# Attention of a fused two-layer kernel: scores issued in pairs, row maxima moved in one hop, query and key rows regrouped in DRAM

## The chip, the cores and the metric

The kernel runs on one core of one Trainium2 chip. The metric is the device time of one execution in microseconds (us), of which a median over several executions is given. All data are float32 at the interface.

## The reference

Two transformer layers with modulated layer norms run over 1024 tokens (2 sequences of 512) of width 256. The change lies in the attention of the first layer, which is this (H = 256, 16 heads of 16):

```python
q_lat = hidden_states @ Wq_down.T + bq_down
kv_lat = hidden_states @ Wkv_down.T + bkv_down
q_half = q_lat @ Wq_up.T + bq_up
q = concatenate([q_half, rotary(q_half)], -1)
k_half = kv_lat @ Wk_up.T + bk_up
k = concatenate([k_half, rotary(k_half)], -1)
v = kv_lat @ Wv_up.T + bv_up
scores = einsum('bhqd,bhkd->bhqk', q, k) / sqrt(16)
out = einsum('bhqk,bhkd->bhqd', softmax(scores), v)
return out.reshape(bsz, seq, H) @ Wo.T + bo
```

After it come a mixture of 16 experts, a gated delta rule (second layer's mixer) and a mixture of 12 experts; the change doesn't touch them.

## The kernel before

The five engines' programs are written out by hand, with semaphores. Attention works in **groups**: group g is 4 heads of one of the 2 sequences, so there are NG = 8 groups. Queries and keys are each split in a high and a low part, so that float32r matmuls keep their precision.

**The rows.** TensorE makes q and k with features on the partitions. `parts_out` (SP queue) writes the high and low parts, four [128, 512] pieces at a time, to the DRAM scratch `part_scratch`. `k_rows` and `q_rows` read them back by head: for a group they fill two tiles [128, 2, 512], Kt and Qt, in which each half of the partitions (`jb` = 0 or 1, from partition 0 or 64) holds two heads, 16 rows to a part (high, low, high for keys; high, high, low for queries), 48 rows in all. A group takes eight such DMAs: four of 32 rows (two parts at once, 128 KB) and four of 16 rows (one part, 64 KB). A row is 4096 bytes. `piece_rows` gives the DRAM side; its pattern is

```python
rows = part_dram[b, n, t // 2, part:part + end - r].rearrange("x (d t o j) n -> (x d) t o (j n)", t=2, j=HP, o=2)
```

where x counts the parts, d the 16 rows of a head, and t, o, j the heads.

**Two score passes.** First pass (`scores`): TensorE makes scores [128 queries, 512 keys] of one head into one of three PSUM banks in turn (`SLOTS`), and VectorE reduces them to a negated maximum per query (`max_of`). There are 16 such scores n to a group, 128 in all. The two halves jb use different rows of the array, and n alternates between them. When a group's 16 maxima are there, VectorE splits them in a bfloat16 high and low part (`mpart`), TensorE turns them (`max_rows`), VectorE copies them to `max_sb`, and the SP queue writes `max_sb` to the DRAM scratch `max_scratch`, waits until that has landed, and reads it back into two more rows of Qt (`maxima_in`). Second pass (`scores_t`): scores with keys on the partitions, in which rows 48 and 49 subtract the maximum; ScalarE takes exp of two heads at once, and TensorE multiplies with the values (`values`).

**The order.** The first FIRST = 26 scores come ahead of everything else; between them stand `up` and `values_in` matmuls and, later, `warm(2, 6)`, two matmuls that do nothing. Then come the groups: each of 8 steps p has a pair of `scores_t`, with the first-pass scores of a later group (`ahead`) between them. `values` of key tile kt come at p = 2 kt + 3. MAX_LAG = 4 says how many scores after a group's last one its `max_rows` stands.

**The SP queue** is written out in the order of the program: the input loads; `parts_out` and the rows of each group; `maxima_in(0)` after the rows of group 2; `maxima_in(1)` after those of group 4; `maxima_in(2)` after those of group 6; then the rows of group 7, the ones rows, `wmod[1]` (1536 KB) and the other `maxima_in`. The rows of query group 0 go by ScalarE's queue.

Of the kernel before, what the change touches and what calls it, by code (L numbers as in the profile page):

```python
# [21 lines left out]
F32 = mybir.dt.float32  # L22
BF16 = mybir.dt.bfloat16
# [6 lines left out]
P = 128  # L30
# [68 lines left out]
FIRST = HG * TB + 10  # L99
MAX_LAG = 4  # L100

# [42 lines left out]
def program(nc, a, out):  # L144
    with ExitStack() as ctx:
        def sb(name, shape, dt=F32):
            return ctx.enter_context(nc.sbuf_tensor(name, shape, dt))
# [38 lines left out]
        small = sb("small", [P, 256])  # L186
        mpart = sb("mpart", [P, 2, 2, NH], BF16)
        max_sb = sb("max_sb", [2 * NH, 2, P])
        ring0 = sb("ring0", [P, 2, W0C])
# [314 lines left out]
        part_dram = nc.dram_tensor("part_scratch", (B, 2, 2, 2, P, S), F32, kind="Internal").ap()  # L504
        max_dram = nc.dram_tensor("max_scratch", (2 * NH, P), F32, kind="Internal").ap()
        ab_dram = nc.dram_tensor("ab_scratch", (2 * NH, TOK), F32, kind="Internal").ap()
# [74 lines left out]
        def piece_rows(n, b, t, r, end, jb):  # L581

            part = (QP, KP)[n][r]
            rows = part_dram[b, n, t // 2, part:part + end - r].rearrange("x (d t o j) n -> (x d) t o (j n)", t=2, j=HP, o=2)
            return rows[:, t % 2, jb]

# [29 lines left out]
        def _(sp):  # L616
# [29 lines left out]
            def maxima_in(g):  # L646

                sp.wait_ge(free_sem(("maxima", g)), uses(("maxima", g)))
                if g:
                    sp.wait_ge(s["max_in"], 32 * g)  # L650
                load("max_out", max_dram, max_sb[:, g % 2, :])
                sp.wait_ge(s["max_out"], 16 * (g + 1))
                for jb in range(2):
                    load("max_in", head_rows(Qt[g // TB][g % TB], jb, KR, KR + 2).bitcast(F32),
                         max_dram.rearrange("(h o j t) q -> h o j (t q)", h=2, j=HP, o=2)[:, jb])

# [23 lines left out]
            for t in (2, 3):  # L680
                ones_rows(sp, 1, t, "ones_late")
            load("ld_mod1", wmod[1], a["wmod"][1])
            for g in range(3, NG):
                maxima_in(g)

            def chunk0(n, k):
# [225 lines left out]
        def _(act):  # L912
# [69 lines left out]
            for g in range(NG):  # L982
                for p in range(2 * TB):
                    act.wait_ge(s["s2"], 2 * TB * g + p + 1)
                    if TB * g + p // 2 >= 2:
                        act.wait_ge(s["av"], TB * g + p // 2 - 1)
                    lo = p // 2 % 2 * HG + p % 2 * 2
                    act.activation(pexp[:, lo:lo + 2, :], psum[:, 2 + p % 2 * 2:4 + p % 2 * 2, :], ACT.Exp,  # L988
                                   scale=HD ** -0.5).then_inc(s["exp"], 1)
                    if g and p == 1:  # L990
                        out_of_psum(g - 1)
                    if (g, p) == (0, 3):
                        high_turned(1)
# [247 lines left out]
        def _(pe):  # L1241
# [77 lines left out]
            def modulate_rows(layer):  # L1319
                pe.wait_ge(s["ld_mod1"], 16 * (layer + 1))  # L1320
                for n in range(2 + layer):
                    for k in range(KD):
                        ins = pe.matmul(bank[MOD_BANKS[layer]][n * Q:n * Q + B, :], ccol[:, layer * KD + k, :],
                                        wmod[layer][:, k, 512 * n:512 * n + 512], start=(k == 0), stop=(k == KD - 1))
                ins.then_inc(s["mod_mm"], 1)
# [61 lines left out]
            def max_rows(g):  # L1387

                pe.wait_ge(s["mpart"], g + 1)
                next_bank("maxima", g)  # L1390
                pe.transpose(bank_b[slot(("maxima", g))][0:2 * NH, 0:P],
                             mpart[:, g % 2, :, :].rearrange("p h n -> p (h n)"), identb[:, :])\
                    .then_inc(full_sem(("maxima", g)), 1)
# [12 lines left out]
            mod_turned(0)  # L1406
            warm(12, 0)
            pe.wait_ge(s["mod_in"], 1)
            for n in range(FIRST):
                scores_and_maxima(n)  # L1410
                if 1 <= n <= 4:
                    if n == 4:
                        pe.wait_ge(s["v_in"], 2)
                    up(1, UP_ORDER[n - 1])
                if n in (6, 8):
                    if n == 8:
                        high_made(pe, 1, 0, 0)
                    values_in(2 + (n - 6) // 2)
                if n >= 10:
                    if n == 10:  # L1420
                        pe.wait_ge(s["up_copy"], 3)
                    warm(2, 6)
            pe.wait_ge(s["up_copy"], 4)
            high_made(pe, 1, 0, 1)
            pe.wait_ge(s["v_in"], NT // 2)
            for g in range(NG):
                for p in range(2 * TB):
                    if p == 0:
                        pe.wait_ge(s["max_in"], 32 * (g + 1))
                        if g == 0:  # L1430
                            pe.wait_ge(s["ones"], 2)
                            pe.wait_ge(s["ones_in"], 16 * 12)
                        if g == TB + 2:
                            pe.wait_ge(s["ones_late"], 64)
# [5 lines left out]
                    if last_maxima_due(g, p):  # L1440
                        max_rows(NG - 1)
                    if p > 1 and p % 2:
                        values(g, p // 2 - 1)
                    elif g and p == 1:
                        values(g - 1, TB - 1)
# [430 lines left out]
        def _(dve):  # L1876
# [105 lines left out]
            def max_of(n):  # L1982
                g, (jj, jb, qt) = n // (HG * TB), head_of(n)
                own, at = nm[:, g % 2, :], (HP * jb + jj) * TB + qt
                dve.tensor_reduce(own[:, at:at + 1], full("scores", n), AX, ALU.max,  # L1985
                                  negate=True).then_inc(free_sem(("scores", n)), 1)
                if n % (HG * TB) == HG * TB - 1:
                    for last in (n - 2, n - 1, n):
                        dve.wait_ge(free_sem(("scores", last)), uses(("scores", last)))
                    ch.link(dve.tensor_copy(mpart[:, g % 2, 0, :], own))  # L1990
                    dve.tensor_tensor(mpart[:, g % 2, 1, :], own, mpart[:, g % 2, 0, :],
                                      ALU.subtract).then_inc(s["mpart"], 1)

            def max_rows(g):
                full("maxima", g)
                if g >= 2:
                    dve.wait_ge(s["max_out"], 16 * (g - 1))
                dve.tensor_copy(max_sb[:, g % 2, :], bank_b[slot(("maxima", g))][0:2 * NH, 0:P])\
                   .then_inc(free_sem(("maxima", g)), 1)

# [691 lines left out]
def lay_out(i):  # L2692
# [15 lines left out]
    up = np.zeros((P, 4, P), f)  # L2708
    turned = np.arange(P).reshape(2, HG, HD).transpose(2, 0, 1).reshape(-1)
    for n, w in enumerate((i["L0_attn_Wq_up"], i["L0_attn_Wk_up"])):  # L2710
# [99 lines left out]
```

## Time and profile before

| | us |
|---|---|
| median of 3 runs | 839.17 |
| lowest and highest | 837.61, 839.66 |
| the profiled execution's own time | 833.2 |
| its span in the profile | 830.9 |
| PE busy | 769.2 (93%) |
| DVE busy | 538.7 (65%) |
| ACT busy | 262.4 (32%) |
| POOL busy | 212.6 (26%) |

The span runs from the first to the last instruction of the profiled execution. PE is TensorE, DVE VectorE, ACT ScalarE, POOL GpSimd; SPq is the queue that issues DMAs. In a timeline row stand the start, the duration of the merged piece, the engine, the line and the operation, and in brackets how long the engine sat idle before it and who ended that. The granted clock of TensorE is 0.96 of full speed over the span. The attention of the first layer lies between about 22 and 160 us.

### The profile page before, as it was taken

How to read it: one execution, taken by the hardware profiler on the slowest of the kernel's cores; microseconds unless marked ns; L12 is line 12 of the kernel's file. 1: busy time of each engine (PE TensorE's matmuls, PEld its weight loads, DVE VectorE, ACT ScalarE, POOL GpSimd, SP SyncE). 2: the span in 40 equal slices, each digit the busy share in tenths (PEclk: the TensorE clock that was granted, in tenths of full speed). 3: DMA queues.
4: the chain of work that ended last, by engine and by line, in shares of the span. 5: the costliest groups of instructions: out<-in, count | busy, mean ns of one | idle time of the engine just before them, and what ended most of it. 6: DMA issues, size and time to landing. Idle time of an engine off the chain costs nothing. (4 is left out here: it accounts for less than half of the span.)

```text
span 830.9 us, 11650 instructions
## 1 busy us (share of the span) xinstructions
PE 769.2 (93%) x4039; PEld 567.0 (68%) x4051; DVE 538.7 (65%) x1312; ACT 262.4 (32%) x417; POOL 212.6 (26%) x202
## 2 busy tenths in 40 slices
PE   8999899999999999999999498998876899999995
PEld 4433343467788888887545387777752899999995
DVE  6577797187655445554789999999478353434345
ACT  2425567534344343433573112021230100000000
POOL 4610000021232222321011000777001253434331
PEclk9998899989999999999999799999987999999997
DMA  7646201001111112131031504400013899999972
GB/s 240 173 131 174 88 4 42 1 23 35 39 57 38 57 38 58 38 117 55 7 108 51 215 1 127 103 0 1 1 52 126 319 345 344 332 354 332 353 256 87
DMA packets 39374, 102.24 MB, mean 123 GB/s; under 512 B 6112, under 2 KB 17632, under 8 KB 38944
## 3 DMA queue, kind: packets, MB, share of 16 engines
q1 hardware_dynamic: 34864, 91.63, 33.0%
q0 software_dynamic: 3888, 9.08, 3.0%
q10 hardware_dynamic: 576, 0.92, 0.4%
q8 instruction: 27, 0.44, 0.2%
q14 instruction: 19, 0.16, 0.1%
HBM read 84.12 MB, written 17.56 MB: 122 GB/s over the span
## 5 line engine op out<-in xcount | busy, mean ns | idle before, releaser
L1494 PE MATMUL psum<-xr,wr 128*128 128x512 f32 x600 | 147.1, 395 | 1.3 <-DVE arena L2144 1.0
L1494 PEld LDWEIGHTS psum<-xr,wr 128*128 128x128 f32 x600 | 114.4, 191 | 26.4 <-issue 2.5
L832 POOL TENSOR_TENSOR wr<-ring,wr 128x512 fp32r<-128x512 f32 (+1 forms) x50 | 54.8, 1115 | 252.1 <-ACT wr L1016 148.3
L1985 DVE TENSOR_REDUCE small<-psum 128x1 f32<-128x512 f32 x128 | 81.4, 684 | 21.9 <-PE psum L1354 21.6
L1810 PEld LDWEIGHTS psum<-arena 128*128 128x128 f32 x700 | 83.5, 192 | 3.2 <-issue 1.5
L1810 PE MATMUL psum<-arena 128*128 128x128 f32 x700 | 83.9, 275 | 1.1 <-ACT arena L1220 1.1
L1820 PE MATMUL psum<-arena 128*128 128x256 f32 x350 | 81.3, 379 | 0.0
L2607 DVE TENSOR_SCALAR arena<-psum,arena 128x256 f32<-128x256 f32 x35 | 16.9, 484 | 94.0 <-PE psum L1820 94.0
L1505 PE MATMUL psum<-hr,wr 128*128 128x512 f32 x300 | 76.6, 391 | 0.9 <-DVE hr L2079 0.9
L988 ACT ACTIVATE arena<-psum 128x1024 f32<-128x1024 f32 x64 | 62.8, 1022 | 44.0 <-PE psum L1363 43.7
L2107 DVE TENSOR_TENSOR hid<-hid,psum 128x512 f32<-128x512 f32 x50 | 34.4, 687 | 57.0 <-ACT hid L1022 56.8
L1820 PEld LDWEIGHTS psum<-arena 128*128 128x128 f32 x350 | 63.8, 190 | 7.2
L1505 PEld LDWEIGHTS psum<-hr,wr 128*128 128x128 f32 x300 | 56.2, 188 | 13.0 <-issue 1.3
L1220 ACT ACTIVATE arena<-psum 128x256 f32<-128x256 f32 x35 | 13.4, 383 | 153.3 <-PE psum L1799 153.3
L2079 DVE TENSOR_TENSOR hr<-hid,hr 128x512 fp32r<-128x512 f32 x50 | 35.0, 700 | 34.0 <-ACT hr L1029 33.8
L1029 ACT ACTIVATE hr<-hid 128x512 fp32r<-128x512 f32 x50 | 31.6, 632 | 78.5 <-DVE hid L2130 68.4
L887 POOL DMA_INDIRECT arena<-h_scratch,arena x35 | 36.2, 1033 | 70.8 <-DVE arena L2580 60.5
L1354 PE MATMUL psum<-k_rows,q_rows 48*128 48x512 f32 x128 | 52.3, 488 | 1.4
L893 POOL DMA_INDIRECT z_scratch<-arena x32 | 31.6, 987 | 81.3 <-DVE arena L2607 81.3
L2639 DVE TENSOR_SCALAR arena<-psum,arena 128x128 f32<-128x128 f32 x175 | 48.2, 342 | 3.6 <-PE psum L1810 3.6
L1363 PE MATMUL psum<-q_rows,k_rows 50*128 50x512 f32 x128 | 42.2, 464 | 3.1 <-DMA q_rows<-max_scratch 2.5
L1269 PE MATMUL psum<-sel,identb 128*128 128x512 bf16 x157 | 43.6, 403 | 0.5 <-issue 0.2
(391 smaller groups left out, 1195.3 us busy)
## 6 DMA issues: line engine op xcount, KB each, us to landing
arena<-in_w1u SPq DMA_DIRECT2D x35, 642.5 KB, 5.8
arena<-in_w1d SPq DMA_DIRECT2D x35, 640.0 KB, 5.5
ring<-in_w SPq DMA_DIRECT2D x25, 384.0 KB, 3.0
part_scratch<-arena SPq DMA_DIRECT2D x16, 256.0 KB, 2.8
z_scratch<-w_a SPq DMA_DIRECT2D x4, 768.0 KB, 7.2
arena<-z_scratch SPq DMA_DIRECT2D x8, 384.0 KB, 6.3
k_rows<-part_scratch SPq DMA_DIRECT2D x16, 128.0 KB, 2.7
qkv_scratch<-arena SPq DMA_DIRECT2D x4, 512.0 KB, 2.8
```

What stands on the lines that cost most here:

```text
L832: pool.tensor_tensor(wr0[:, k, LO, part], ring0[:, k, part], wr0[:, k, HI, part], ALU.subtract).then_inc(s["w0_lo"], 1)
L887: pool.indirect_dma_start(xg[:, r % NXG, :], None, h_dram, bass.IndirectOffsetOnAxis(ap=tok_i[:, r:r + 1], axis=0))\
L988: act.activation(pexp[:, lo:lo + 2, :], psum[:, 2 + p % 2 * 2:4 + p % 2 * 2, :], ACT.Exp, scale=HD ** -0.5).then_inc(s["exp"], 1)
L1269: pe.matmul(bank[spare][:, :], identb[:, :], sel0[:, :], start=True, stop=True)
L1354: pe.matmul(to, head_rows(Qt[b][t], jb, 0, KR)[:, jj, tile(qt)], head_rows(Kt[b][t], jb, 0, KR)[:, jj, :], start=True, stop=True)\
L1363: ins = pe.matmul(bank[2 + 2 * pair + jb][:, :], head_rows(Kt[b][t], jb, 0, KR + 2)[:, pair, tile(kt)], head_rows(Qt[b][t], jb, 0, KR + 2) ...
L1494: ins = pe.matmul(bank[2 * b + m][:, :], wr0[:, k, w, lo:lo + P], xr[:, x, f, half(b)], start=(f == 0 and (w, x) == PARTS[0]), stop=(f == ...
L1505: ins = pe.matmul(bank[4 + 2 * m + b][:, :], wr0[:, k, w, lo:lo + P], hr[:, b, x, :], start=(first and (w, x) == PARTS[0]), stop=(last and ...
L1810: ins = pe.matmul(bank[2 + r % 2 * 3 + k // 2][:, tile(k % 2)], wup1[:, r % NW, lo:lo + P], xgT[:, r % 2, f, :], start=(f == 0), stop=(f = ...
L1820: ins = pe.matmul(bank[1][:, 0:D], hact[:, r % 2, tile(k)], wdn1[:, r % NW, k * D:(k + 1) * D], start=(k == 0), stop=(k == NC1 - 1))
L1985: dve.tensor_reduce(own[:, at:at + 1], full("scores", n), AX, ALU.max, negate=True).then_inc(free_sem(("scores", n)), 1)
L2639: ins = dve.tensor_scalar(hact[:, r % 2, tile(k)], bank[2 + r % 2 * 3 + k // 2][:, tile(k % 2)], bias, 0.0, ALU.add, ALU.max)
```

## The change

It has five parts.

- The first 26 scores come in pairs n, n + 1 (the two halves of the array), with one `up` or `values_in`, or three `warm` matmuls, after each pair; `warm(12, 0)` ahead of them becomes `warm(6, 0)`, and the wait for `mod_in` moves to n = 4.
- The maxima are turned in float32 straight from `nm`, VectorE writes the high and low part from PSUM to `max_sb`, and four DMAs (half by part) carry them from SBUF to Qt. `max_scratch` and its wait are gone; MAX_LAG is 3.
- The features are ordered anew in the weights (`turned`, in `lay_out`), so that the two heads of one half lie in 64 KB without gaps per part in `part_scratch`.
- `values` of key tile kt come at p = 2 kt + 2, between the two halves of the next key tile, and `out_of_psum` one step earlier.
- `wmod[1]` is loaded in two halves, after `maxima_in(3)` and `maxima_in(4)`.

```diff
-MAX_LAG = 4
+MAX_LAG = 3
...
-        mpart = sb("mpart", [P, 2, 2, NH], BF16)
-        max_sb = sb("max_sb", [2 * NH, 2, P])
+        max_sb = sb("max_sb", [NH, 2, 2, P], F32R)
...
-            rows = part_dram[b, n, t // 2, part:part + end - r].rearrange("x (d t o j) n -> (x d) t o (j n)", t=2, j=HP, o=2)
-            return rows[:, t % 2, jb]
+            rows = part_dram[b, n, t // 2, part:part + end - r].rearrange("x (t o d j) n -> x d t o (j n)", t=2, j=HP, o=2)
+            return rows[:, :, t % 2, jb]
...
                 if g:
-                    sp.wait_ge(s["max_in"], 32 * g)
-                load("max_out", max_dram, max_sb[:, g % 2, :])
-                sp.wait_ge(s["max_out"], 16 * (g + 1))
+                    sp.wait_ge(s["max_in"], 64 * g)
                 for jb in range(2):
-                    load("max_in", head_rows(Qt[g // TB][g % TB], jb, KR, KR + 2).bitcast(F32),
-                         max_dram.rearrange("(h o j t) q -> h o j (t q)", h=2, j=HP, o=2)[:, jb])
+                    for part in (HI, LO):
+                        load("max_in", head_rows(Qt[g // TB][g % TB], jb, KR + part, KR + part + 1)
+                             .rearrange("p j n -> p (j n)").bitcast(F32),
+                             max_sb[jb * NH // 2:(jb + 1) * NH // 2, g % 2, part, :].bitcast(F32))
...
-            load("ld_mod1", wmod[1], a["wmod"][1])
             for g in range(3, NG):
                 maxima_in(g)
+                if g - 3 < KD:
+                    load("ld_mod1", wmod[1][:, g - 3], a["wmod"][1, :, g - 3])
...
-                    if g and p == 1:
+                    if g and p == 0:
                         out_of_psum(g - 1)
...
             def max_rows(g):
-                pe.wait_ge(s["mpart"], g + 1)
-                next_bank("maxima", g)
-                pe.transpose(bank_b[slot(("maxima", g))][0:2 * NH, 0:P],
-                             mpart[:, g % 2, :, :].rearrange("p h n -> p (h n)"), identb[:, :])\
+                for n in range(HG * TB * (g + 1) - 3, HG * TB * (g + 1)):
+                    pe.wait_ge(free_sem(("scores", n)), uses(("scores", n)))
+                pe.transpose(next_bank("maxima", g)[0:NH, 0:P], nm[:, g % 2, :], ident[:, :])\
                     .then_inc(full_sem(("maxima", g)), 1)
...
-            warm(12, 0)
-            pe.wait_ge(s["mod_in"], 1)
-            for n in range(FIRST):
+            warm(6, 0)
+            for n in range(0, FIRST, 2):
                 scores_and_maxima(n)
-                if 1 <= n <= 4:
+                scores_and_maxima(n + 1)
+                if n < 8:
...
-                    warm(2, 6)
+                    warm(3, 6)
...
-                    if p > 1 and p % 2:
+                    if p and p % 2 == 0:
                         values(g, p // 2 - 1)
-                    elif g and p == 1:
+                    elif g and p == 0:
                         values(g - 1, TB - 1)
...
             def max_rows(g):
-                full("maxima", g)
+                turned = full("maxima", g)[0:NH, 0:P]
                 if g >= 2:
-                    dve.wait_ge(s["max_out"], 16 * (g - 1))
-                dve.tensor_copy(max_sb[:, g % 2, :], bank_b[slot(("maxima", g))][0:2 * NH, 0:P])\
-                   .then_inc(free_sem(("maxima", g)), 1)
+                    dve.wait_ge(s["max_in"], 64 * (g - 1))
+                ch.link(dve.tensor_copy(max_sb[:, g % 2, HI, :], turned))
+                dve.tensor_tensor(max_sb[:, g % 2, LO, :], turned, max_sb[:, g % 2, HI, :].bitcast(F32),
+                                  ALU.subtract).then_inc(free_sem(("maxima", g)), 1)
...
-    turned = np.arange(P).reshape(2, HG, HD).transpose(2, 0, 1).reshape(-1)
+    turned = np.arange(P).reshape(2, 2, HP, HD).transpose(0, 1, 3, 2).reshape(-1)
```

On the SP queue, this is what stands between the row DMAs of group 2 (k_rows_59, q_rows_51) and of group 3 (k_rows_60) before; the shapes are those of the destination:

```order
L602 DMA k_rows_59<-part_scratch 32x1024
L602 DMA k_rows_59<-part_scratch 16x1024
L602 DMA k_rows_59<-part_scratch 32x1024
L602 DMA k_rows_59<-part_scratch 16x1024
L608 DMA q_rows_51<-part_scratch 16x1024
L608 DMA q_rows_51<-part_scratch 32x1024
L608 DMA q_rows_51<-part_scratch 16x1024
L608 DMA q_rows_51<-part_scratch 32x1024
L618 DMA max_scratch<-max_sb 32x128
L618 DMA q_rows_49<-max_scratch 2x1024 x2
L602 DMA k_rows_60<-part_scratch 32x1024
```

and in the changed kernel:

```order
L600 DMA k_rows_59<-part_scratch 32x1x1024
L600 DMA k_rows_59<-part_scratch 16x1024
L600 DMA k_rows_59<-part_scratch 32x1x1024
L600 DMA k_rows_59<-part_scratch 16x1024
L606 DMA q_rows_51<-part_scratch 16x1024
L606 DMA q_rows_51<-part_scratch 32x1x1024
L606 DMA q_rows_51<-part_scratch 16x1024
L606 DMA q_rows_51<-part_scratch 32x1x1024
L616 DMA q_rows_49<-max_sb 1x8x128 x4
L600 DMA k_rows_60<-part_scratch 32x1x1024
```

The place of the maxima of group 0 (q_rows_49) is the same, behind the rows of group 2. The DMAs of 32 rows have one more dimension, since x and d no longer make one stride: the DRAM side is now 2 parts, 65536 elements apart, of 16 rows, 1024 elements apart; before it was 32 rows, 4096 elements apart. The 16-row DMAs read 16 adjacent rows.

On TensorE, two key tiles of group 2 (keys k_rows_59; L1363 is `scores_t`, L1354 `scores`, L1376 `values`) before:

```order
L1363 MATMUL psum<-q_rows_51,k_rows_59 128x512
L1354 MATMUL psum<-k_rows_60,q_rows_52 128x512
L1363 MATMUL psum<-q_rows_51,k_rows_59 128x512
L1354 MATMUL psum<-k_rows_60,q_rows_52 128x512
L1363 MATMUL psum<-q_rows_51,k_rows_59 128x512
L1354 MATMUL psum<-k_rows_60,q_rows_52 128x512
L1363 MATMUL psum<-q_rows_51,k_rows_59 128x512
L1354 MATMUL psum<-k_rows_60,q_rows_52 128x512
L1376 MATMUL psum<-arena 17x512 x4
```

and in the changed kernel (L1362, L1353 and L1375 are the same three):

```order
L1362 MATMUL psum<-q_rows_51,k_rows_59 128x512
L1353 MATMUL psum<-k_rows_60,q_rows_52 128x512
L1362 MATMUL psum<-q_rows_51,k_rows_59 128x512
L1353 MATMUL psum<-k_rows_60,q_rows_52 128x512
L1375 MATMUL psum<-arena 17x512 x4
L1362 MATMUL psum<-q_rows_51,k_rows_59 128x512
L1353 MATMUL psum<-k_rows_60,q_rows_52 128x512
L1362 MATMUL psum<-q_rows_51,k_rows_59 128x512
L1353 MATMUL psum<-k_rows_60,q_rows_52 128x512
```

`values` moved from behind both halves of a key tile to between them; what it multiplies is the exp of the key tile before.

## Rows read from the trace of the kernel before

**Rows 1.** The head of the page.

```profile
span 830.9 us, 11650 instructions
```

**Rows 2.** Timeline, TensorE: the first scores_t (L1363) of groups 0 to 6.

```profile
54.03 0.49 PE L1363 MATMUL psum<-q_rows,k_rows 50*128 50x512 f32 x1
...
68.67 0.50 PE L1363 MATMUL psum<-q_rows,k_rows 50*128 50x512 f32 x1
...
81.33 0.49 PE L1363 MATMUL psum<-q_rows,k_rows 50*128 50x512 f32 x1 [0.69 <-DMA q_rows<-max_scratch]
...
95.07 0.50 PE L1363 MATMUL psum<-q_rows,k_rows 50*128 50x512 f32 x1 [1.80 <-DMA q_rows<-max_scratch]
...
109.26 0.49 PE L1363 MATMUL psum<-q_rows,k_rows 50*128 50x512 f32 x1
...
122.08 0.50 PE L1363 MATMUL psum<-q_rows,k_rows 50*128 50x512 f32 x1
...
133.98 0.50 PE L1363 MATMUL psum<-q_rows,k_rows 50*128 50x512 f32 x1
```

**Rows 3.** One line's instructions, VectorE L1985 from 29 to 54 us, and its idle time.

```profile
L1985 DVE TENSOR_REDUCE small<-psum x26: 678/691/692, 30.0 to 53.6; 128x1 f32<-128x512 f32 x26
...
  PE psum L1354: 8.9, 18
```

**Rows 4.** Timeline, the SP queue: start, us, line, DMAs.

```profile
22.26 8.80 SPq L602 DMA_DIRECT2D k_rows<-part_scratch  x8
...
48.55 0.30 SPq L618 DMA_DIRECT2D max_scratch<-max_sb  x1
49.94 0.55 SPq L618 DMA_DIRECT2D q_rows<-max_scratch  x2
...
85.41 0.40 SPq L618 DMA_DIRECT2D arena<-in_wmod  x1
88.98 0.33 SPq L618 DMA_DIRECT2D max_scratch<-max_sb  x1
93.18 0.52 SPq L618 DMA_DIRECT2D q_rows<-max_scratch  x2
```

**Rows 5.** What the SP queue waited for, 20 to 145 us: in total, times, longest.

```profile
SPq L618 <- DMA max_scratch<-max_sb: 13.1, 8, 3.9
...
SPq L602 <- DMA q_rows<-part_scratch: 5.4, 1, 5.4
```

**Rows 6.** DMA issues: queue, count, KB each, median us to landing where told.

```profile
k_rows<-part_scratch SPq DMA_DIRECT2D x16, 128.0 KB, 2.7
...
q_rows<-max_scratch SPq DMA_DIRECT2D x16, 8.0 KB
k_rows<-hid POOLq DMA_DIRECT2D x12, 8.0 KB, 5.4
...
k_rows<-hid SPq DMA_DIRECT2D x4, 8.0 KB
```

**Rows 7.** Stretches; the last three columns are PEclk, DMA share, GB/s.

```profile
50.98:51.15 0.17, 0.17 (x2) 0.02 (x1) 0.17 (x1) 0.00 (x0) 0.00 (x0) 1.00 0.12 50
50.98:51.38 0.40, 0.40 (x2) 0.18 (x1) 0.40 (x1) 0.00 (x0) 0.00 (x0) 1.00 0.13 41
52.00:53.00 1.00, 1.00 (x4) 0.30 (x3) 0.72 (x2) 0.00 (x0) 0.00 (x0) 1.00 0.74 205
56.00:57.00 1.00, 1.00 (x5) 0.58 (x5) 1.00 (x3) 1.00 (x2) 0.00 (x0) 1.00 1.05 402
...
96.00:102.50 6.50, 6.50 (x28) 2.04 (x25) 4.67 (x10) 4.31 (x5) 0.00 (x0) 0.50 0.00 0
```

**Rows 8.** Timeline of the first key tile of group 5: exp, values, next scores_t.

```profile
122.85 1.94 ACT L988 ACTIVATE arena<-psum 128x1024 f32<-128x1024 f32 x2 [0.76 <-PE psum L1363]
...
123.80 1.05 PE L1376 MATMUL psum<-arena 128*17 128x512 f32 x8
...
124.78 0.50 PE L1363 MATMUL psum<-q_rows,k_rows 50*128 50x512 f32 x1
```

More of the change, by code:

```diff
@@ L504, in program @@
         part_dram = nc.dram_tensor("part_scratch", (B, 2, 2, 2, P, S), F32, kind="Internal").ap()
-        max_dram = nc.dram_tensor("max_scratch", (2 * NH, P), F32, kind="Internal").ap()
         ab_dram = nc.dram_tensor("ab_scratch", (2 * NH, TOK), F32, kind="Internal").ap()
@@ L1319, in modulate_rows @@
             def modulate_rows(layer):
-                pe.wait_ge(s["ld_mod1"], 16 * (layer + 1))
+                pe.wait_ge(s["ld_mod1"], 16 * (1 + KD * layer))
                 for n in range(2 + layer):
@@ L1406, in _ @@
             mod_turned(0)
-            warm(12, 0)
-            pe.wait_ge(s["mod_in"], 1)
-            for n in range(FIRST):
+            warm(6, 0)
+            for n in range(0, FIRST, 2):
                 scores_and_maxima(n)
-                if 1 <= n <= 4:
+                scores_and_maxima(n + 1)
+                if n < 8:
                     if n == 4:
+                        pe.wait_ge(s["mod_in"], 1)
+                    if n == 6:
                         pe.wait_ge(s["v_in"], 2)
-                    up(1, UP_ORDER[n - 1])
-                if n in (6, 8):
-                    if n == 8:
+                    up(1, UP_ORDER[n // 2])
+                elif n < 12:
+                    if n == 10:
                         high_made(pe, 1, 0, 0)
-                    values_in(2 + (n - 6) // 2)
-                if n >= 10:
-                    if n == 10:
+                    values_in(2 + (n - 8) // 2)
+                else:
+                    if n == 12:
                         pe.wait_ge(s["up_copy"], 3)
-                    warm(2, 6)
+                    warm(3, 6)
             pe.wait_ge(s["up_copy"], 4)
@@ L1428, in _ @@
                     if p == 0:
-                        pe.wait_ge(s["max_in"], 32 * (g + 1))
+                        pe.wait_ge(s["max_in"], 64 * (g + 1))
                         if g == 0:
@@ L1986, in max_of @@
                                   negate=True).then_inc(free_sem(("scores", n)), 1)
[L1987 to L1992, printed above, removed]
             def max_rows(g):
-                full("maxima", g)
+                turned = full("maxima", g)[0:NH, 0:P]
                 if g >= 2:
-                    dve.wait_ge(s["max_out"], 16 * (g - 1))
-                dve.tensor_copy(max_sb[:, g % 2, :], bank_b[slot(("maxima", g))][0:2 * NH, 0:P])\
-                   .then_inc(free_sem(("maxima", g)), 1)
+                    dve.wait_ge(s["max_in"], 64 * (g - 1))
+                ch.link(dve.tensor_copy(max_sb[:, g % 2, HI, :], turned))
+                dve.tensor_tensor(max_sb[:, g % 2, LO, :], turned, max_sb[:, g % 2, HI, :].bitcast(F32),
+                                  ALU.subtract).then_inc(free_sem(("maxima", g)), 1)
             def normalise(g):
```

## The prediction

> **What bounds the kernel now.** I read the timeline first, because the change lies in one stage. The span is 830.9 us [rows 1], and the first `scores_t` of the groups stand at 54.0, 68.7, 81.3, 95.1, 109.3, 122.1 and 134.0 us [rows 2]. What the reader should see is the spacing: group 5 takes 133.98 - 122.08 = 11.90 us with nothing to wait for, groups 2 and 3 begin after waits of 0.69 and 1.80 us for the maxima from DRAM, and group 3 takes 14.19 us, since from 96 to 102.5 us the granted clock was 0.50 [rows 7], that is 1.2 GHz, after the idle 1.80 us. So a restart at the low clock costs 14.19 - 11.90 = 2.3 us. Ahead of group 0 lie 26 single scores, 29.5 to 54.0 us; VectorE needs 0.69 us for each and sat idle 8.9 us between them, waiting for scores [rows 3]. TensorE bounds that stretch and the groups. All that follows attention only starts later or earlier with it.
>
> The transfers are next. The rows of group 0 are issued at 22.26 us, and the SP queue waits 5.4 us for them before it issues those of group 1 [rows 4, 5]. The maxima of group 0 go out at 48.55 us, 1.39 us later the queue may read them back, and their first bytes move at 50.98 us, 1.04 us after that issue [rows 4, 7]. In the case of group 3 the first hop took from 88.98 to 93.18 us, 4.2 us, because 1536 KB had been issued at 85.41 us [rows 4]: a small transfer stands behind the large ones ahead of it on its queue. That matters below.
>
> **The part that decides: how many DMA engines a row transfer gets.** In rows 7 the stretch 50.98 to 51.38 us holds only the two reads of maxima, each of two rows of 4096 bytes. The DMA share is 0.13, which is 2 engines of 16, and 41 GB/s: the two rows of a transfer go side by side on two engines, and the second transfer goes after the first on the same two, though 14 are free. These transfers, and the ones rows from the SP queue, are also the only ones for which no landing time is told, while those from GpSimd's queue have one [rows 6]; I read this as another number of completions than 16. So a transfer is dealt out once, by its outermost count. The 32-row transfers had the outermost count 32 on both sides. After the change x and d make no single stride, and the DRAM side is 2 x 16 rows, outermost count 2. The trace has no transfer of 32 rows in two blocks. The bounds are 2 engines (nearest in outermost count) and 16 (nearest in size). I take 2, since the two reads behind one another show that size and free engines play no role.
>
> The Trainium skill, "DMA: Bandwidth & Descriptors", section "Why a DMA increments its semaphore by 16 and not by 1", says that a DMA runs on the largest number up to 16 that divides the slowest dimension of both sides, on hardware queues the lowest-numbered engines. By that rule 32-row transfers get 2 engines and the sum below holds; without it the first rival does. This case's 0.13 of 16 agrees as far as it goes.
>
> **Price of a row.** On two engines 50 GB/s gives 25 GB/s each, 0.164 us for 4096 bytes; over both transfers 41 GB/s gives 0.20; in the contended stretch 52 to 53 us 205 GB/s on 0.74 x 16 engines gives 0.24 [rows 7]. I take 0.165 us, the uncontended one, since 14 engines will be mostly idle; 0.20 is kept for the range. One group: four 32-row transfers put 16 rows on each of the two engines, four 16-row ones put 1 row: 68 x 0.165 = **11.2 us**. One `parts_out` of 4 x 128 rows of 2048 bytes puts 32 rows on each; 402 GB/s on 1.05 x 16 engines gives 0.086 us a row [rows 7]: **2.75 us**. An issue takes 1.05 us to its first row, and a landing about 0.3 us (estimate).
>
> **The sum**, along the SP queue's order. Group 0's rows: 22.26 + 1.04 + 11.2 = 34.5, landed 34.8 (before, some 29.4 by the 5.4 us wait). Group 1's, first row 35.9, done 47.1; parts of the other head pair behind them 49.8, landed 50.1. Group 2's rows 51.2 to 62.4; the maxima of group 0, behind them, 62.7, so group 0 begins at 62.7 instead of 54.0. Group 3's rows 73.6, parts 76.4 (landed 76.7), group 4's rows 77.7 to 88.9, maxima of group 1 at 89.2 (68.7 before). Parts 91.7, group 5's rows 102.9, group 6's 114.1, **maxima of group 2 at 114.4 instead of 81.3: +33.1 us**. TensorE has by then stood idle some 12 us and restarts at 1.2 GHz: group 2 takes 11.9 + 2.3 = 14.2 and ends at 128.6; group 7's rows are in at 125.3 and the maxima of group 3 at 125.6, so group 3 begins at 128.6, +33.5. From there no row is owed. Group 3 before held a low-clock restart that now has no cause: -2.3. So +31.2.
>
> The other parts. **Pairs** would save TensorE time in the first 26 scores, but these now wait for rows and maxima: 0. **One hop** saves 1.4 us a group and the two waits of 0.69 and 1.80 us; groups 0 to 2 wait for the queue instead, and group 3's wait is gone in the sum already: 0. VectorE loses two small operations a group and gains one in another place: 0, hidden behind TensorE, worth at most some 0.2 us a group. `max_rows` at MAX_LAG 3 stands inside a pair and holds up one `scores_t` by up to one reduction, 0.6 us a group at most, 0 at least; taken as 0. **wmod** in halves is behind maxima: 0. **Values between the halves**: exp starts 0.77 us after its half's first matmul (122.08 to 122.85) and takes 0.97 [rows 2, 8], ready 1.75 us after it; two halves of four matmuls occupy TensorE 1.72 us (122.08 to 123.80), and values 0.98 (to 124.78). Values used to find their exp ready; now they wait for the half just before, so a key tile takes 1.80 + 0.98 = 2.78 instead of 2.70. Over some 14 key tiles +1.1; in the last group and a half, where no first-pass scores fill the halves, about 0.3 us for each of 6 tiles. I take +2 (0 to 4).
>
> Sum: 31.2 + 2 = **+33 us** on the profiled execution's 833.2 (span 830.9), so 866. That execution was 6.0 us under the median 839.17; on the median the forecast is **872 us**.
>
> **Rivals.**
> - *All 16 engines work on the 2 x 16 rows (the other side: faster).* Then the rows stay hidden. Pairs bring the first 26 scores to VectorE's pace [rows 3], 26 x 0.69 = 17.9 instead of 24.6 us: -6.7; the waits -0.69 and -1.80; the restart -2.3; values +2: -9.5, so **830 us**. It decides at about four engines: 4 x 8 + 4 = 36 rows, 5.9 us a group, is already less than a group's 11.9. For it: TensorE idles nowhere in the trace for rows of this size, and 128 KB landed in 2.7 us [rows 6]. Against it: the two-row stretch. 12%.
> - *Two engines, but the maxima overtake.* They use eight partitions and could travel on other engines. Then only the rows count: group 4's at 88.9 are needed in group 2, group 7's at 125.3 in group 5; groups 0 and 1 start late by 4 to 8 us, and little is regained: about **843 us**. Against it: the 4.2 us of group 3's first hop. 5%.
> - *Two engines, slow rows.* At 0.20 us, 0.035 x 68 x 7 groups = +17 more: **889 us**; at 0.24, 908. Rows read side by side could be as slow as in the second read of maxima. I count 0.20 as the edge of the forecast's own range, and 5% beyond.
> - The forecast itself: 78%, with its own range 856 to 890.
>
> **How the numbers follow.** The likeliest case gives 872. The range 854 to 892 leaves out the first two rivals and the slowest rows. A measurement of this kernel can tell about 0.3%, 2.5 us, from no change. Faster: the first rival, 0.12. Same: a remainder between the first two, 0.02. Slower: 0.86.
>
> **What would show it.** Right: between 24 and 125 us the DMA share near 0.13, and some 45 to 50 GB/s; the SP queue waits over 10 us for group 0's rows; TensorE's first `scores_t` at about 63, 89, 114 and 129 us, the waits put down to `q_rows<-max_sb`, granted clock 0.50 after each; from group 3 on the spacing of before, about 12 us; key tiles of 2.8 instead of 2.7 us. The 32-row transfers should have no landing told. Wrong: 32-row transfers that land in 3 us and groups that begin ahead of 54 us. If rows take 11 us a group and the maxima land early all the same, the queue order was misread.

## The result, and the profile after

The changed kernel took **882.1 us** (median of 4 runs, 879.26 to 883.69), the kernel before 838.39 (4 runs, 831.53 to 839.66). The ratio is 1.0535, 95% interval 1.0471 to 1.0599. The profiled execution took 881.46 us with a span of 879.2, beside 833.2 and 830.9 [rows 1]: +48.3 us. The forecast was 872 on the median, +33 on the profiled execution: the right sign and mechanism, 10 us short on the median and 15 us on the execution.

The head of its page, and the granted clock and the DMA share in 40 slices of 22 us each, in tenths:

```profile
span 879.2 us, 11628 instructions
...
PEclk8785568999899999999999979999996999999997
DMA  6222311010011111111303150430001799999973
```

Slices 4 to 6, 66 to 132 us, hold the clock's dip (5, 5, 6): groups 0 to 2 of attention. Behind attention only single slices stand at 7 or 6, three of them; the page of before has three such slices too (7). I then read the same views in the same order as before. First the timeline of TensorE (start, us, engine, line, operation; behind it the idle time and what ended it), for the first `scores_t` of groups 0, 1, 2 and 3 and the last one of all:

```profile
70.51 0.76 PE L1362 MATMUL psum<-q_rows,k_rows 50*128 50x512 f32 x1 [9.26 <-DMA q_rows<-max_sb]
...
98.10 0.79 PE L1362 MATMUL psum<-q_rows,k_rows 50*128 50x512 f32 x1 [12.13 <-DMA q_rows<-max_sb]
...
124.31 0.79 PE L1362 MATMUL psum<-q_rows,k_rows 50*128 50x512 f32 x1 [11.23 <-DMA q_rows<-max_sb]
...
140.73 0.40 PE L1362 MATMUL psum<-q_rows,k_rows 50*128 50x512 f32 x1
...
202.12 0.50 PE L1362 MATMUL psum<-q_rows,k_rows 50*128 50x512 f32 x2
```

Against [rows 2] group 0 is 16.5 us late, group 1 29.4, group 2 43.0, group 3 45.7. Three waits for `q_rows<-max_sb` hold 32.6 us; behind group 3 nothing is owed. From group 3 to the last `scores_t` it is 61.4 us; before, it was 57.7 (95.07 to 152.73), so 3.7 us more come there. 45.7 + 3.7 = 49.4 at the end of attention, 48.3 at the end of the program: the rest only moved.

The waits of TensorE and of the SP queue (in total, times, longest), 20 to 170 us:

```profile
PE psum L1362 <- DMA q_rows<-max_sb: 32.6, 3, 12.1
...
PE psum L1353 <- DMA q_rows<-part_scratch: 7.5, 1, 7.5
```
```profile
SPq L616 <- DVE max_sb L1993: 29.3, 4, 10.4
SPq L600 <- DMA part_scratch<-arena: 22.7, 4, 9.1
SPq L600 <- DMA q_rows<-part_scratch: 11.2, 1, 11.2
```

The queue waits 11.2 us for group 0's rows, where it waited 5.4 [rows 5]. Stretches (length; busy us and count of PE, PEld, DVE, ACT and POOL; granted clock, DMA share, GB/s):

```profile
11.00:18.00 7.00, 5.72 (x12) 2.71 (x12) 3.60 (x10) 1.45 (x2) 0.00 (x0) 0.51 0.59 171
...
28.50:37.50 9.00, 2.34 (x12) 0.97 (x10) 0.17 (x1) 1.41 (x3) 2.49 (x2) 0.86 0.13 53
...
35.00:48.00 13.00, 9.59 (x15) 3.14 (x16) 4.44 (x7) 3.22 (x5) 3.05 (x3) 0.50 0.37 129
...
68.00:104.00 36.00, 21.34 (x81) 8.29 (x85) 13.76 (x24) 12.18 (x14) 2.50 (x2) 0.50 0.33 116
...
121.00:137.00 16.00, 12.66 (x49) 4.53 (x49) 6.72 (x12) 5.61 (x6) 0.00 (x0) 0.50 0.11 44
```

The second of these stretches, 28.5 to 37.5 us, is the main one: only rows move, at a DMA share of 0.13, two engines of 16, and 53 GB/s: 26.5 GB/s each, 0.155 us for a row of 4096 bytes. TensorE meanwhile has nothing to do for some 7 us (31 to 38 us). And each wait is paid for twice, with the idle time and with slow work behind it: the clock is 0.50 (1.2 GHz) from 35 to 48, 68 to 104 and 121 to 137 us.

### The profile page after: what moved, and what is told of

It reads as the page before. It is cut to its first block and busy times, and to the rows that moved or that the text cites. A ratio compares the mean times of both kernels' runs of the same rounds, so it can differ in the third digit from the quotient of the medians.

```text
span 879.2 us, 11628 instructions
## 1 busy us (share of the span) xinstructions
PE 780.0 (89%) x4034; PEld 569.9 (65%) x4034; DVE 537.1 (61%) x1304; ACT 262.4 (30%) x417; POOL 212.8 (24%) x202
## 5 line engine op out<-in xcount | busy, mean ns | idle before, releaser
L1985 DVE TENSOR_REDUCE small<-psum 128x1 f32<-128x512 f32 x128 | 80.3, 682 | 63.5 <-PE psum L1353 63.4
L1362 PE MATMUL psum<-q_rows,k_rows 50*128 50x512 f32 x128 | 47.9, 510 | 32.6 <-DMA q_rows<-max_sb 32.6
L1362 PEld LDWEIGHTS psum<-q_rows,k_rows 50*128 50x128 f32 x128 | 23.3, 220 | 64.0 <-DMA q_rows<-max_sb 24.5
L1353 PE MATMUL psum<-k_rows,q_rows 48*128 48x512 f32 x128 | 54.9, 550 | 8.3 <-DMA q_rows<-part_scratch 7.5
L2634 DVE TENSOR_SCALAR arena<-psum,arena 128x128 f32<-128x128 f32 x175 | 48.3, 342 | 3.7 <-PE psum L1810 3.7
```

The costliest lines, as they stand in the source:

```text
L1353: pe.matmul(to, head_rows(Qt[b][t], jb, 0, KR)[:, jj, tile(qt)], head_rows(Kt[b][t], jb, 0, KR)[:, jj, :], start=True, stop=True)\
L1362: ins = pe.matmul(bank[2 + 2 * pair + jb][:, :], head_rows(Kt[b][t], jb, 0, KR + 2)[:, pair, tile(kt)], head_rows(Qt[b][t], jb, 0, KR + 2) ...
L2634: ins = dve.tensor_scalar(hact[:, r % 2, tile(k)], bank[2 + r % 2 * 3 + k // 2][:, tile(k % 2)], bias, 0.0, ALU.add, ALU.max)
```

## The experiments

Eleven kernels ran, one of them twice, in four sets, each beside runs of the kernel before on the same chip. The medians of before were 837.4, 839.2, 837.4 and 837.9 us; each ratio is to the one of its own set, and between sets the ratios compare better than the medians.

### Which part costs: the layout undone, transfers split, the layout alone

**old_layout**: the changed kernel with the DRAM layout of before.

```
-  rearrange("x (t o d j) n -> x d t o (j n)", ...); rows[:, :, t % 2, jb]
+  rearrange("x (d t o j) n -> (x d) t o (j n)", ...); rows[:, t % 2, jb]
-  turned = np.arange(P).reshape(2, 2, HP, HD).transpose(0, 1, 3, 2)
+  turned = np.arange(P).reshape(2, HG, HD).transpose(2, 0, 1)
```

> The changed kernel with one part undone: the parts lie in DRAM as before, so that a row transfer of 32 rows has one outermost count of 32 again; one hop for the maxima, pairs, and values between the halves stay. Theory (the number of DMA engines of the row transfers is the whole cause): about 832 us (830 from the first rival of the prediction, and the values between the halves may cost 2 more), the DMA share over 0.5 while rows arrive, and the first scores_t of groups 0 to 3 near 49 to 54, 63 to 67, 76 to 80 and 89 to 93 us. Rival 1 (the maxima in four small transfers from SBUF to SBUF are slow by themselves, 2.7 us for their issues): the groups still wait for q_rows<-max_sb, 845 us or more. Rival 2 (values between the halves cost a lot): key tiles stay at 2.85 us and the total is about 838 to 842.

836.1 us, ratio 0.9993 (0.9963 to 1.0023). The whole loss is gone, and so the layout is its cause (with what it makes of the transfers; the next kernel parts the two); but nothing is gained either, where 832 was expected. The trace says why:

```profile
49.23 0.47 PE L1362 MATMUL psum<-q_rows,k_rows 50*128 50x512 f32 x1 [0.57 <-DMA q_rows<-max_sb]
...
65.04 0.79 PE L1362 MATMUL psum<-q_rows,k_rows 50*128 50x512 f32 x1 [5.05 <-DMA q_rows<-max_sb]
...
81.45 0.40 PE L1362 MATMUL psum<-q_rows,k_rows 50*128 50x512 f32 x1
```
```profile
55.77 0.28 DVE L1993 TENSOR_TENSOR max_sb<-psum,max_sb 16x128 fp32r<-16x128 f32 x1
...
56.40 1.72 SPq L600 DMA_DIRECT2D k_rows<-part_scratch  x4
58.16 2.90 SPq L606 DMA_DIRECT2D q_rows<-part_scratch  x4
61.19 2.69 SPq L616 DMA_DIRECT2D q_rows<-max_sb  x4
```

Group 0 begins 4.8 us earlier than before, as the pairs promise. But group 1's maxima, in SBUF at 56.05 us, are issued at 61.19, behind eight row loads for group 4, and their four issues take 2.7 us where the two reads of before took 0.55 [rows 4]. TensorE waits 5.05 us and runs group 1 at the low clock. That is rival 1 of the expectation in another form: the maxima go out late, by their place and by the length of their issues. The transfers themselves are not slow, TensorE goes 1.2 us after the end of the last issue (63.88 us). What the place of the values costs, rival 2, comes below.

**split_16**: the contiguous layout stays; every 2 x 16-row transfer goes out as two of 16 rows.

```
-KRUN = ((0, 2), (2, 3))          QRUN = ((0, 1), (1, 3))
+KRUN = ((0, 1), (1, 2), (2, 3))  QRUN = ((0, 1), (1, 2), (2, 3))
```

> The changed kernel, its contiguous DRAM layout kept, but each transfer of two parts (2 x 16 rows) is issued as two transfers of 16 rows, twelve a group instead of eight. Theory (outermost count 2 is the cause, not the layout): within 2 us of the kernel with the old layout, about 832 us; four more issues a group at about 0.55 us each on the SP queue, 2.2 us, are hidden. Rival (contiguous rows in DRAM are slow to read, whatever the number of engines): stays at about 882 us, or clearly above 850. Rival (the queue's issue time becomes the bound): 835 to 840 us, with groups 0 to 2 late by 2 to 4 us.

841.8 us, ratio 1.0042 (1.0014 to 1.0070). 40 of the 44 us are gone with the layout in place: it is not contiguous DRAM that is slow, it is the form 2 x 16. The remaining 5.7 us over old_layout fit the third theory: the SP queue issues from 48.6 to 71.0 us with only some 1.4 us of waits, and the maxima of group 1 go out at 68.28 instead of 61.19. Of these 7.1 us, 2.2 are a later start of this execution (its first `part_scratch` issue stands at 21.12 us against 18.91; see the last section), so some 5 are the queue's.

**before_new_layout**: the kernel before with the layout alone (the same two edits, the other way round).

> The kernel before with one part of the change alone: the contiguous DRAM layout, whose 32-row transfers have 2 x 16 rows. Theory (this part alone makes the loss): 878 to 890 us, since the maxima still go out to DRAM and come back, each hop behind rows that run on two engines; the difference to the kernel before is 40 to 50 us. Rival (the loss comes from the layout together with the four small transfers of the maxima, or with the new place of the values): under 865 us.

895.0 us, ratio 1.0697 (1.0641 to 1.0753): +57.6, above the expected 878 to 890. Here both hops of the maxima stand behind two-engine rows: group 1's go out at 91.39 us and may be read back only at 101.04.

```profile
91.39 0.33 SPq L618 DMA_DIRECT2D max_scratch<-max_sb  x1
101.04 0.52 SPq L618 DMA_DIRECT2D q_rows<-max_scratch  x2
```

So the change's other parts together are worth some 13 us beside this layout, and as a whole they add nothing to the loss. The 9.7 us between these two rows are a hop that the change doesn't have, so I take most of the 13 us to be that hop; no run has it alone.

### How the loss grows with the rows on the fullest engine

**split_q_only** applies the `QRUN` edit alone. A group then has two transfers of 2 x 16 rows and eight of 16 rows (two for the keys, six for the queries): 2 x 16 + 8 = 40 rows on each of the two fullest engines. The expectations here and for blocks_8 say 38; they left the keys' own 16-row transfers out.

> The changed kernel with only the query side's transfers of two parts issued as two of 16 rows; the key side's stay 2 x 16. A group then puts 2 x 16 + 6 = 38 rows on each of the two lowest engines instead of 68, about 6.3 to 7.2 us at 0.165 to 0.19 us a row, less than the 12 us of a group's work. Theory (there is a threshold: rows cost only what does not fit beside a group's work; the prediction put it at about 36 rows): worked along the SP queue, maxima of group 1 at about 71 us instead of 67, of group 2 at about 87 instead of 84, nothing owed from there on: 838 to 846 us. Rival (the loss is proportional to the rows on the fullest engine): 882 minus 30/64 of about 48, which is 859 us.

855.6 us, ratio 1.0224 (1.0175 to 1.0274). **blocks_8** lays the parts out in between, with 4 blocks `h` of 4 dimensions `d`:

```
-  rearrange("x (t o d j) n -> x d t o (j n)", ...)
+  rearrange("x (h t o d j) n -> (x h) d t o (j n)", ..., h=4)
-  turned = ....reshape(2, 2, HP, HD).transpose(0, 1, 3, 2)
+  turned = ....reshape(2, 2, HP, 4, HD // 4).transpose(3, 0, 1, 4, 2)
```

> The changed kernel with a DRAM layout between the two: the 16 dimensions of a head in 4 blocks of 4, heads between the blocks. A 32-row transfer has an outermost count of 8 (blocks of 4 rows), a 16-row transfer one of 4. Theory of the outermost count: 8 and 4 engines work, 4 rows each, so a group puts 32 rows on the fullest engine (68 in the change, 38 in split_q_only, 12 in old_layout), and the DMA share while rows run is 0.25 to 0.5. If the loss is proportional to the rows on the fullest engine (836 at 12, 855.6 at 38, 882 at 68, so 0.8 us a row): 852 us. If there is a threshold near 36 rows, as the prediction had it: 838 to 842 us. If a transfer runs either on two engines or on all: 836 or 882 us.

846.6 us, ratio 1.0074 (1.0039 to 1.0109), and in its stretches, while rows are the only transfers:

```profile
30.50:31.00 0.50, 0.50 (x4) 0.20 (x3) 0.17 (x1) 0.40 (x1) 0.50 (x1) 1.00 0.43 156
31.50:32.00 0.50, 0.37 (x2) 0.00 (x0) 0.00 (x0) 0.00 (x0) 0.50 (x2) 1.00 0.22 82
```

0.43 and 0.22 of 16 engines are some 7 and 3.5 engines. From 29.5 to 32.5 us all half microseconds lie between 0.22 and 0.43, so neither two engines nor all; I read them as 8 and 4 with gaps, which is what outermost counts of 8 and 4 give. The Trainium skill, "DMA: Bandwidth & Descriptors", section "Why a DMA increments its semaphore by 16 and not by 1", takes the largest number up to 16 that divides the slowest dimension of both sides; the 0.13 of the changed kernel agrees, and these two shares fit it.

The series, by rows of a group on the fullest engine, is 12 rows 836.1 us, 32 rows 846.6, 40 rows 855.6, 68 rows 882.1. That is 0.53 us a row between the first two, 1.1 in the next step (two more issues a group are in it) and 0.95 in the last. (blocks_8 ran in a set whose kernel before was 1.7 us slower; by the ratios the first two steps are 0.34 and 1.6.) 846.6 lies between the two theories, 852 and 842, and split_q_only at 855.6 is far nearer to the proportional 859 than to the threshold's 838 to 846. **The prediction took anything under 36 rows a group to be free, and that is wrong**: at 32 rows the ratio is 1.0074 against 0.9993 at 12, with intervals that don't meet. Rows that fit beside a group's 12 us still delay the start of groups 0 to 2, for there each link waits for the one before: rows, first-pass scores, maxima, and these behind the next rows. In blocks_8 TensorE waits 0.4, 10.2 and 3.1 us for the maxima of groups 0, 1 and 2 and not for those of group 3, in split_q_only 6.8, 5.0 and 5.2 us.

**new_layout_maxima_first** asks whether the place of the maxima in the queue alone could hide slow rows. On SP, in the changed kernel:

```
             load("ld_g", consts[:, :], a["consts"])
+            maxima_in(1)
             parts_there(1, 0)
             both_rows(1, 0)
-            maxima_in(1)
...
             both_rows(1, 1)
+            maxima_in(2)
             parts_there(1, 1)
             both_rows(1, 2)
-            maxima_in(2)
             both_rows(1, 3)
```

> The changed kernel, its row transfers on two engines, with only the order of the SP queue changed: maxima of group 1 ahead of the rows of group 4, maxima of group 2 ahead of the rows of group 6. Theory (most of the loss in groups 1 and 2 is the maxima's place behind 12 to 14 us of rows that nobody needs yet, not the rows themselves): group 1 begins near 86 us instead of 98 and group 2 near 100 to 105 us instead of 124, total 858 to 866 us. Rival (rows themselves are needed as they come): under 5 us of gain, 877 us or more.

878.6 us, ratio 1.0459 (1.0414 to 1.0503): my theory fell. Its first half holds, group 1 begins at about 83.9 us, 14 earlier than in the change. Then

```profile
111.85 0.79 PE L1362 MATMUL psum<-q_rows,k_rows 50*128 50x512 f32 x1 [15.37 <-DMA q_rows<-max_sb]
...
135.32 0.79 PE L1362 MATMUL psum<-q_rows,k_rows 50*128 50x512 f32 x1 [9.90 <-DMA q_rows<-max_sb]
```

group 2 and group 3 wait the longer, since their maxima stand behind all the rows that were passed over: those of group 3 are issued at 122.37 us, behind the rows of group 7. So group 3 begins at 135.3 us, only 5.4 earlier than in the change (140.7, where it didn't wait), and groups 3 to 7 need 62.6 us behind it instead of 61.4. With slow rows the order of the queue moved the wait and hardly shortened it: 3.5 us by the medians, 6 by the ratios.

### The place of the values, and a version that beats both

**old_layout_values_back** is old_layout with the values behind both halves again, on TensorE and, for what leaves PSUM, on ACT:

```
-                    if p and p % 2 == 0:
+                    if p > 1 and p % 2:
                         values(g, p // 2 - 1)
-                    elif g and p == 0:
+                    elif g and p == 1:
                         values(g - 1, TB - 1)
...
-                    if g and p == 0:
+                    if g and p == 1:
                         out_of_psum(g - 1)
```

> The kernel with the old DRAM layout, and the values again after both halves of the next key tile (PE and ACT order of before); one hop, pairs and MAX_LAG 3 stay. Theory (the place of the values costs time from group 3 on: 61.3 us from group 3's start to the last scores_t in old_layout against 57.7 before, with 3.3 us of PE waits for the exp): that stretch falls back to about 57.7 us, total 832.5, 3.6 us under old_layout. Rival (the longer stretch comes from max_rows standing inside a pair at MAX_LAG 3, or from the four issues of the maxima): the stretch stays at about 61 us, total 836.

831.0 us, ratio 0.9905 (0.9869 to 0.9941): 5.1 us under old_layout, in two different sets (7.4 by the ratios). Group 3's start to the last `scores_t` is 54.9 us (89.60 to 144.50) instead of 61.3. Before, it was 57.7 with a restart of 2.3 in it, so the new place costs some 6 us. The same stretch is 54.9 us in all three variants of the change with the values behind the halves, and 60.8 to 62.6 us in the change and its six variants with the values between them. The last group shows it best; first the changed kernel, then this one:

```profile
191.57 1.05 PE L1375 MATMUL psum<-arena 128*17 128x512 f32 x8 [0.36 <-ACT arena L987]
...
193.62 0.50 PE L1362 MATMUL psum<-q_rows,k_rows 50*128 50x512 f32 x2
194.48 1.05 PE L1375 MATMUL psum<-arena 128*17 128x512 f32 x8 [0.36 <-ACT arena L987]
...
196.33 1.02 ACT L987 ACTIVATE arena<-psum 128x1024 f32<-128x1024 f32 x1 [0.98 <-PE psum L1362]
```
```profile
136.98 1.05 PE L1375 MATMUL psum<-arena 128*17 128x512 f32 x8
...
138.83 1.94 ACT L987 ACTIVATE arena<-psum 128x1024 f32<-128x1024 f32 x2
...
139.47 1.05 PE L1375 MATMUL psum<-arena 128*17 128x512 f32 x8
```

From `values` to `values`, a key tile takes 2.91 us against 2.49. Between the halves the values wait 0.36 us for exp, and exp then waits 0.98 us for the half behind the values: each engine waits for the other once a tile.

**maxima_first_values_back** adds the SP order of new_layout_maxima_first to it.

> As old_layout_values_back, and on the SP queue the maxima of groups 1 and 2 are moved ahead of the row loads of groups 4 and 6. Theory (in old_layout group 1's maxima are in SBUF at 56.0 us but issued at 61.2 us behind eight row loads, TensorE idles 5.0 us and restarts at 1.2 GHz, about 4 us more in that group): both go, group 1 begins near 61.5 us and group 2 near 74 us, total about 825 us (822 to 829), under both kernels. Rival (something else delays group 1, for instance the four issues of 0.65 us each and their landing): group 1 begins at 64 us or later and the total stays at 830 us or more.

**822.5 us, ratio 0.9800 (0.9766 to 0.9834)**, under both kernels. A second measurement, **best_again**:

> maxima_first_values_back a second time. All theories: 822 to 826 us, ratio 0.98 to 0.985 to the kernel before. If the first measurement had mostly caught executions whose start ran at the full clock, 825 to 827 us. Its profile should show group 0 at 48 to 57 us, the earlier value when the granted clock is 1.00 from 11 to 18 us.

823.4 us (819.38 to 825.96), ratio 0.9808 (0.9776 to 0.9840). TensorE's and SP's rows of that profile:

```profile
PE psum L1362 <- DMA q_rows<-max_sb: 1.8, 3, 0.6
PE psum L1353 <- DMA q_rows<-part_scratch: 1.5, 1, 1.5
```
```profile
59.66 3.02 SPq L616 DMA_DIRECT2D q_rows<-max_sb  x4
62.72 1.82 SPq L600 DMA_DIRECT2D k_rows<-part_scratch  x4
```

The maxima go ahead of group 4's rows, group 1 begins at 64.91 us, no wait is over 0.6 us for them, and attention's last `scores_t` is at 144.94 us, 7.8 us earlier than before. The profiled executions differ by 8.1 us (825.09 and 833.2), the medians by 14.5; no trace shows where the rest arises.

What the new queue order brings beside old_layout_values_back is 8.5 us by the medians of one set. Their traces don't show it: the profiled execution of old_layout_values_back was its fastest (824.87 us); there TensorE waited only 0.78 us for group 1's maxima, and its last `scores_t` stands at 144.50 us. So the gain is measured and its way, fewer waits for maxima, is argued.

Three more kernels take this version apart.

**before_pairs** is the kernel before with the change's loop over the first 26 scores:

```
-            for n in range(FIRST):
-                scores_and_maxima(n)
+            for n in range(0, FIRST, 2):
+                scores_and_maxima(n)
+                scores_and_maxima(n + 1)
...
```

> The kernel before with one part of the change alone: its first 26 scores go out in pairs, the other TensorE work of that stretch between the pairs. The prediction priced pairs at 6.7 us if nothing else binds (26 reductions at VectorE's 0.69 us instead of 24.6 us). Theory: group 0 begins 5 to 6 us earlier (54.0 to about 48.5 us), groups 1 and 2 then wait more for their maxima, which stand behind eight row loads and take two hops; 1 to 4 us are left at the end, 834 to 837 us beside 838. Rival (all of it arrives): 832 us.

835.8 us, ratio 0.9977 (0.9947 to 1.0007). Nothing that can be told apart. In the trace group 0 begins 1.4 us earlier than before, though this execution started 3.6 us later (first `part_scratch` issue at 21.55 us against 17.99), and the groups then wait longer for their maxima, 0.88, 1.96 and 1.08 us for groups 1 to 3 against 0, 0.69 and 1.80 [rows 2].

**best_singles** is maxima_first_values_back with that loop of before, one score at a time.

> maxima_first_values_back without the pairs: its first 26 scores one at a time as before, so the rest is one hop and the new queue order. Theory (the 16.7 us under the kernel before come from pairs, 6, from the maxima's one hop and place, 4 to 6, and from restarts at 1.2 GHz that fall away, 2 to 4, and these add up): 828 to 830 us. Rival (pairs bring nothing since the later groups regain it): 823 us; other rival (only pairs count): 837 us.

830.3 us, ratio 0.9907 (0.9875 to 0.9939). So pairs are worth some 7 to 8 us here, and at most some 4 in the kernel before (the interval's lower end): a gain at the front arrived only in the kernel in which the next wait had been moved too.

**maxima_first** is maxima_first_values_back with the values between the halves, the edit above undone.

> maxima_first_values_back with the values between the halves again. Theory (their place costs 3.5 to 5 us, by old_layout against old_layout_values_back): 826 to 828 us against 822.5. Rival (with the maxima early the place of the values does not matter): 823 us.

830.3 us, ratio 0.9911 (0.9875 to 0.9947), 7 to 8 us over it. Their place matters, whether the maxima are early or not.

## Why the prediction was right in direction and short in size

- **Two engines for 2 x 16 rows: right.** Share 0.13, 53 GB/s, and undoing it by layout or by splitting takes the loss away. The sign that I gave, a share near 0.13 from 24 to 125 us, holds only where rows move alone; over that whole stretch it is 0.27, since other transfers run in it. That all missing landing times would mark such transfers was a poor sign: the 64 KB transfers of 16 rows had none in the changed kernel either, yet split_16 shows them to be fast.
- **0.165 us a row: right when rows move alone (0.155), short along the path.** Group 0 was forecast at 62.7 and began at 70.5. Of these 7.8 us, 2.4 are a late start (SP's first row issue at 24.66 us instead of 22.26, with the granted clock at 0.51 from 11 to 18 us, where [rows 4]'s execution had 1.00). The other 5.4 are rows: group 2's are issued at 54.55 us, forecast 50.1, and the maxima behind them let TensorE go at 70.51, 16.0 us later, where 12.6 were forecast. The next two groups took 27.6 and 26.2 us against 26.5 and 25.2. In all 7.5 us. Spread over the 7 x 68 rows on that way it would be 0.18 us a row instead of 0.165, and 0.21 in group 2's part (3.4 us over 68 rows), where several transfers are under way; I had 0.20 as an edge. Whether the rows themselves are slower there or the issues and landings around them was not settled.
- **Group 2 at the low clock: 16.4 us instead of 14.2.** I took the cost of one restart from a group that had waited 1.8 us. Here the clock stayed at 0.50 until 137 us, and TensorE was busy only 12.7 of the 16 us. +2.2.
- **Values between the halves: the term that was most wrong.** Forecast +2 (0 to 4), though its own two terms, 1.1 and 6 x 0.3, add up to 2.9; measured about 6 by the stretch behind group 3, 5.1 and 7.8 by medians. I had priced the wait of TensorE for exp and not ACT's wait for TensorE behind it. The 2.3 us saved on group 3's restart were right in kind (12.4 us against 14.2), so the net was +3.7 and not -0.3: +4.0.
- Together 2.4 + 7.5 + 2.2 + 4.0 = 16.1 us at the end of attention, of which 15 reach the end of the program. The 2.4 us are chance in that execution and no part of the mechanism (see the last section). On the median it is 10 us, since the profiled execution of before was faster than its median.
- **Pairs, one hop, halves of wmod: 0.** No run shows these terms alone in the changed kernel. The sum follows the changed kernel's own queue, so that the missing hop stands in it already: it lacks none of the 13 us by which before_new_layout is slower. But without it two-engine rows would have cost 57.6 us instead of 43.7, which the prediction nowhere says.
- **The rival of 16 engines: 830 forecast, 836 measured** (old_layout). It lacked the issue time of the four maxima (2.7 us), the rows ahead of them, and the true price of the values. Its decision point, 36 rows, was wrong, as blocks_8 and split_q_only show. The rival in which the maxima overtake falls too: in the change those of group 0, issued from 59.00 to 61.73 us, let TensorE go only at 70.51, 8.8 us after the last issue ends, where it is 1.2 us in old_layout. Its 843 us no run tests; with the maxima of groups 1 and 2 alone ahead in the queue it is 878.6.

## What to carry to other kernels

A change of layout that makes bytes contiguous can take engines away from a transfer: look at the outermost dimension of both sides as the instruction carries it, and split the transfer rather than let that count fall to 2. Put small transfers that somebody waits for ahead of large ones that nobody needs yet, but check what then stands behind them; with slow rows it mostly moved the wait. And a gain at the front of a chain (pairs) counts only after the next link has been freed: the same edit was worth 0 to 4 us in one kernel and 7 to 8 in another.

## What the runs showed that I had not expected

- **The start has two levels.** From 11 to 18 us the granted clock was 1.00 in eight of the 14 profiled executions (before, old_layout, split_q_only, new_layout_maxima_first, old_layout_values_back, best_again, best_singles, maxima_first) and 0.51 to 0.60 in six (the change, split_16, before_new_layout, blocks_8, maxima_first_values_back, before_pairs). The first `part_scratch` issue stood at 17.91 to 19.53 us in the eight and at 20.40 to 21.55 us in the six. It doesn't belong to a program: best_again and maxima_first_values_back are one and the same, and the first has 1.00, group 0 at 51.47 us and a span of 822.8, the second 0.51, 57.13 and 827.6. So of the 48 us between the two main profiles some 2.4 are this. A part of the spread of all kernels (before: 830.5 to 841.9 us in the 23 runs of the first set) may be that; only profiled executions show it, so it is not shown for the others.
- **A busy TensorE can be at 1.2 GHz.** In old_layout_values_back the clock fell while TensorE worked, after 0.66 us of idle time in the four microseconds before:

```profile
46.00:50.00 4.00, 3.34 (x17) 1.43 (x15) 3.48 (x7) 1.18 (x2) 0.00 (x0) 1.00 0.42 117
50.00:54.00 4.00, 4.00 (x16) 1.52 (x16) 3.46 (x6) 3.28 (x5) 0.00 (x0) 0.64 0.97 282
54.00:60.00 6.00, 6.00 (x27) 2.70 (x24) 3.19 (x7) 2.50 (x3) 2.50 (x2) 0.50 0.61 177
```

  In old_layout the same stretch, with 0.57 us of idle time from 46 to 50 us, kept 1.00. What decides between them is open.
- **Issues cost by form.** Four SBUF-to-SBUF issues of eight rows of 512 bytes take 2.7 us on SP, 0.67 each, against 0.27 for each read from DRAM that they replace [rows 4]. In split_16, which has four more row issues a group as well, the SP queue issues almost without a pause ahead of group 1's maxima.
